# Expert and shared matrices laid out turned ahead of the launch and loaded into place, in a graph layer with routed experts

## The reference, cut to what matters

```python
def _L0_ffn_ref(x, gate_w, w1, w2, w3, sw1, sw2):      # 8 experts, 512 -> 256 -> 512
    logits = xf @ gate_w.T                             # one expert a token, weight 1
    h = silu(einsum('nd,eid->nei', xf, w1)) * einsum('nd,eid->nei', xf, w3)
    y = einsum('nei,edi->nd', h * comb[:, :, None], w2)
    y = y + gelu(xf @ sw1.T) @ sw2.T                   # the shared part
```

## Time and profile before

| | |
|---|---|
| median of 3 runs | 2850.24 us (2848.74 to 2852.52) |
| the profiled execution: span from first to last instruction | 3300.0 us |
| mean granted TensorE clock over the span | 0.919 |
| busy shares: PE, DVE, POOL, ACT | 77%, 67%, 46%, 22% |
| `route_and_share` in the trace | from 2964.3 us to the first gather of the experts at 3115.8 |
| `run_experts` in the trace | from 3115.8 us to the end |

### The profile page before, as it was taken

One profiled execution on the slowest core, in us unless ns is written; L12 is line 12 of the kernel. 1 busy time (PEld: TensorE's weight loads), 2 busy tenths in 40 slices (PEclk: granted clock), 3 DMA queues, 4 the chain that ended last, 5 costly groups with the idle time before them and its releaser, 6 DMA issues. The chain is left out here.

```text
span 3300.0 us, 44711 instructions
## 1 busy us (share of the span) xinstructions
PE 2528.1 (77%) x13652; PEld 1568.7 (48%) x13652; DVE 2222.5 (67%) x3894; ACT 731.3 (22%) x1526; POOL 1531.5 (46%) x1568
## 2 busy tenths in 40 slices
PE   3999894888888878888784067877877777887798
PEld 2565543555555555555553034444444444446443
DVE  7578543777777777777777967676766767775222
ACT  1333311333333333333332010000000000004321
POOL 2232203555555555555552056666655665641144
PEclk7999997999999999999997578988888888889899
DMA  3112227666666666666666045656555565654443
GB/s 125 47 60 63 73 93 134 175 177 174 174 173 175 177 173 174 174 175 176 174 173 205 34 143 168 176 167 173 168 166 171 164 173 164 177 149 154 133 128 94
DMA packets 180188, 490.81 MB, mean 149 GB/s; under 512 B 39490, under 2 KB 52194, under 8 KB 178942
## 3 DMA queue, kind: packets, MB, share of 16 engines
q0 software_dynamic: 117200, 384.69, 41.9%
q1 hardware_dynamic: 48468, 77.23, 7.7%
q10 hardware_dynamic: 14298, 26.03, 2.5%
HBM read 440.04 MB, written 49.72 MB: 148 GB/s over the span
## 5 line engine op out<-in xcount | busy, mean ns | idle before, releaser
L1078 POOL DMA_INDIRECT rows_v<-target_rows,edge_dst x672 | 682.6, 1016 | 682.8 <-ACT edge_terms L1184 423.7
L1405 PE MATMUL ps_sum<-messages,node_onehot 128*125 128x512 f32 x1344 | 806.7, 694 | 232.3 <-DVE messages L1381 221.5
L1360 POOL DMA_INDIRECT rows_e<-message_rows,edge_dst x672 | 635.7, 946 | 552.0 <-issue 204.7
L1095 DVE TENSOR_TENSOR rows_v<-rows_v,ps_u 128x520 f32<-128x520 f32 x672 | 451.3, 693 | 328.0 <-PE ps_u L1127 175.4
L1127 PE MATMUL ps_u<-edge_space,source_onehot_t 125*128 x4032 | 535.5, 277 | 55.5 <-DVE rows_v L1095 37.0
L1178 ACT ACTIVATE w_abs<-ps_w 128x1024 f32<-128x1024 f32 x336 | 344.2, 1024 | 845.8 <-remote 558.4
L1142 PE MATMUL ps_w<-ident,rows_v 128*128 128x128 f32 x2688 | 362.4, 278 | 212.3 <-ACT w_abs L1178 212.3
L1109 DVE SCALAR_TENSOR_TENSOR w_abs<-w_abs,corner 128x512 f32<-128x512 f32 x672 | 474.0, 746 | 0.9 <-ACT w_abs L1178 0.9
L1142 PEld LDWEIGHTS ps_w<-ident,rows_v 128*128 128x128 f32 x2688 | 292.4, 142 | 358.8 <-DVE rows_v L1095 280.6
L1127 PEld LDWEIGHTS ps_u<-edge_space,source_onehot_t 125*128 125x128 bf16 x4032 | 378.7, 97 | 152.4 <-issue 75.8
L1406 PEld LDWEIGHTS ps_den<-edge_space,node_onehot 128*125 128x125 f32 x1344 | 273.6, 204 | 368.8 <-issue 368.8
(11 more groups left out here) (404 smaller groups left out, 2366.7 us busy)
## 6 DMA issues: line engine op xcount, KB each, us to landing
edge_ids<-local_ids ACTq DMA_DIRECT2D x84, 250.0 KB
edge_space<-in_L_ffn_w_dram SPq DMA_DIRECT2D x24, 512.0 KB, 4.3
rows_v<-target_rows,edge_dst POOLq DMA_INDIRECT x672
scores<-score SPq DMA_DIRECT2D x672, 16.0 KB
rows_e<-message_rows,edge_dst POOLq DMA_INDIRECT x672
source_parts<-edge_space SPq DMA_DIRECT2D x20, 380.9 KB
edge_space<-source_parts SPq DMA_DIRECT2D x4, 1904.3 KB
scores<-score SPq DMA_DIRECT2D x336, 8.0 KB
```

Source lines behind the costliest of these rows:

```text
L1078: nc.gpsimd.indirect_dma_start(rows[q][:, j, :], None, tab_v, bass.IndirectOffsetOnAxis(ap=edge["dst"][:, tile:tile + 1], axis=0)).then_in ...
L1095: v.tensor_tensor(w[q % RING][:, j, :].rearrange("p (a b) -> p a b", a=2), rows[q % RING][:, j, :].rearrange("p (a b) -> p a b", a=2), ps_ ...
L1360: nc.gpsimd.indirect_dma_start(rows[q][:, j, :], None, tab_e, bass.IndirectOffsetOnAxis(ap=edge["dst"][:, tile:tile + 1], axis=0)).then_in ...
L1405: nc.tensor.matmul(ps_sum[h][:, :], onehot[h][:, j, :], messages[h][:, j, :], start=j == 0, stop=j == GROUP - 1)
```

## The change

`kernel()` now calls `lay_out`, which turns the six kinds of matrices before the launch and hands them over as four arrays: `up` (`w1` and `w3` side by side), `down`, `gate_up` (gate and `sw1` side by side) and `shared_down`, each with the partition first. In `route_and_share` SP loads them straight into the tiles that the products read: 27 loads become 8, of which the two of `down` wait until `sums`, whose space they take, has been used up. `turn_matrix` and `keep_matrix` are gone with their PSUM banks and places. PE waits for `gate_up` ahead of its first tile and for `shared_down` ahead of the second loop's first product; `run_experts` waits for all six expert loads (`experts_in`) between turning its first tile and the first product. The factor one half moves from the copies of `w2` to DVE's second gating operation, which changes its form for it.

```diff
         @block.sync
         def _(sp):
-            sp.dma_start(gate_rows, a["L0_ffn_gate_w"]).then_inc(s["gate_in"], 16)
-
-            def load(m):
-                name, e = MATRICES[m]
-                if m >= RAWS:
-                    sp.wait_ge(weights_turned, m - RAWS + 1)
...
-                sp.dma_start(rows, whole.rearrange("(k p) f -> p k f", p=P)).then_inc(loaded[m % RAWS], 16)
...
+            sp.dma_start(ffn["gate_up"][:, :, :], a["gate_up"]).then_inc(s["gate_up_in"], 16)
+            sp.dma_start(ffn["shared_down"][:, :, :], a["shared_down"]).then_inc(s["shared_in"], 16)
+            for k in range(KF):
+                sp.dma_start(ffn["up"][:, k, :, :], a["up"][:, k, :, :]).then_inc(experts_in, 16)
+            sp.wait_ge(s["sums_used"], NC)
+            for e in range(0, EXPERTS, EXPERTS // 2):
+                sp.dma_start(ffn["down"][:, e:e + EXPERTS // 2, :, :], a["down"][:, e:e + EXPERTS // 2, :, :]).then_inc(experts_in, 16)
+            sp.wait_ge(s["shared_in"], 16)
...
-            def turn_matrix(m):
-                pe.wait_ge(loaded[m % RAWS], 16 * (m // RAWS + 1))
-                if m >= 2:
-                    pe.wait_ge(weights_kept, m - 1)
-                for half in range(IH):
-                    for k in range(KF):
-                        at = k * INNER + half * P if wide(m) else half * F + k * P
-                        ins = t_.transpose(ps_w[2 * (m % 2) + half][:, k * P:(k + 1) * P], raw[m % RAWS][:, at:at + P], ident[:, :])
-                ins.then_inc(weights_turned, 1)
...
-            pe.wait_ge(s["gate_in"], 16)
-            for k in range(KF):
-                ins = t_.transpose(ps_gate[:, k * EXPERTS:(k + 1) * EXPERTS], gate_rows[:, k * P:(k + 1) * P], ident[0:EXPERTS, 0:EXPERTS])
-            ins.then_inc(s["gate_turned"], 1)
-            for m in range(BEFORE):
-                turn_matrix(m)
+            pe.wait_ge(s["gate_up_in"], 16)
...
-            act.wait_ge(s["gate_turned"], 1)
-            sc.copy(ffn["gate_up"][:, :, 0:EXPERTS], ps_gate[:, 0:KF * EXPERTS].rearrange("p (k e) -> p k e", k=KF))
-            for m in range(2):
-                keep_matrix(m)
-            for m in range(2, BEFORE):
-                keep_matrix(m)
             deviate(0)
...
-                v.tensor_tensor(hidden[:, :], ps_up[:, INNER:2 * INNER], gate[:, :], ALU.mult).then_inc(s["hidden_set"], 1)
+                v.scalar_tensor_tensor(hidden[:, :], ps_up[:, INNER:2 * INNER], 0.5, gate[:, :], ALU.mult, ALU.mult).then_inc(s["hidden_set"], 1)
...
             turn(0)
+            pe.wait_ge(experts_in, 16 * (KF + 2))
             up(0)
...
+def lay_out(inputs, np):
+    def turned(name):
+        return np.moveaxis(inputs[name], -1, 0)
+
+    def chunks(one):
+        return one.reshape((-1, P) + one.shape[1:]).swapaxes(0, 1)
+    up = np.concatenate([turned('L0_ffn_w1'), turned('L0_ffn_w3')], axis=2)
+    gate_up = np.concatenate([turned('L0_ffn_gate_w'), turned('L0_ffn_sw1')], axis=1)
+    down = np.moveaxis(chunks(turned('L0_ffn_w2')), 2, 1)
+    laid = {name: inputs[name] for name in _INS}
+    laid.update(up=chunks(up), gate_up=chunks(gate_up), down=down, shared_down=chunks(turned('L0_ffn_sw2')))
+    return laid
```

More of the change, by code:

```diff
@@ L1422, in _, with route_and_share @@
             in_turns(TURNS, ((0, lay_weights),), TURN)
[L1425 removed]
+def route_and_share(nc, a, const, ffn, x_sb, sums, denominators, spare, raw_space, idle, tokens, tab_x, tab_r, residual_out, experts_in):
     ident, tri, ones, row, eps = (const[k] for k in ("ident", "tri", "ones", "row", "eps"))
@@ L1508, in ps_h @@
             return ps_xt[(t - LISTED_AT) % 2 if t >= LISTED_AT + 2 else 1]
-        def matrices_at(first, last, step, steps):
-            share = last - first
-            return range(first + share * step // steps, first + share * (step + 1) // steps)
         @block.sync
         def _(sp):
-            sp.dma_start(gate_rows, a["L0_ffn_gate_w"]).then_inc(s["gate_in"], 16)
-            def load(m):
-                name, e = MATRICES[m]
-                if m >= RAWS:
-                    sp.wait_ge(weights_turned, m - RAWS + 1)
-                whole = a[name][e, :, :] if name in ("L0_ffn_w1", "L0_ffn_w2", "L0_ffn_w3") else a[name]
-                rows = raw[m % RAWS].rearrange("p (k i) -> p k i", k=KF) if wide(m) else raw[m % RAWS].rearrange("p (i f) -> p i f", f=F)
-                sp.dma_start(rows, whole.rearrange("(k p) f -> p k f", p=P)).then_inc(loaded[m % RAWS], 16)
-            for m in range(RAWS):
-                load(m)
-            for m in range(RAWS, len(MATRICES)):
-                load(m)
+            sp.dma_start(ffn["gate_up"][:, :, :], a["gate_up"]).then_inc(s["gate_up_in"], 16)
[6 more added lines that the diff above has]
+            sp.wait_ge(s["shared_in"], 16)
         @block.gpsimd
@@ L1821, in _, with run_experts @@
                         gelu(t + 2)
-                    for m in matrices_at(AT_COUNT + 3, len(MATRICES), t, NB):
-                        keep_matrix(m)
-def run_experts(nc, const, ffn, tokens, tab_x, tab_r, residual_out, out):
+def run_experts(nc, const, ffn, tokens, tab_x, tab_r, residual_out, experts_in, out):
     ident = const["ident"]
@@ L2040 @@
     arrays, args = {}, {}
-    for name in _INS:
-        a = _np.ascontiguousarray(inputs[name])
+    for name, laid in lay_out(inputs, _np).items():
+        a = _np.ascontiguousarray(laid)
         arrays[f"in_{name}_dram"] = a
```

62 lines of the change are left out of this document (10 added, 52 removed).

## The result

The changed kernel takes 2824.82 us (median of 4 runs, 2823.87 to 2825.24), the kernel before, run beside it, 2850.99 (4 runs, 2848.74 to 2852.52): a ratio of 0.991, 95% interval 0.9898 to 0.9922, or 26.2 us gained where 20.4 were forecast. The forecast of 2829.8 us is 5 us too high; its range of 2824.5 to 2839 holds the result by 0.3 us. It was right on the direction and on most of the steps. That the range holds is luck: its terms at their best gave 25.1 us, or 2825.1 us, and the result lies beyond that. Behind the missing 5 us stand errors with opposite signs. Writes that were held up cost some 3.6 us where nothing was taken. The half clock, which costs the kernel before more than its one trace showed and the change less than before, gave some 8 us that were not counted: some 2 in the start and 6 in the first loop. Smaller differences make up the rest.

What follows compares the result with a forecast made beforehand. The stage was taken as bound by a late start, an ACT-DVE-PE ring, DVE's routing, then PE in the second loop. 5.5 - 1.0 + 5.8 + 0.9 - 0.5 + 9.7 = 20.4 us off 2850.24 gives 2829.8, range 2824.5 to 2839.

Steps and rivals of the forecast that it cites:

- The start: Start of the stage: without the matrices' turning ahead of it, the first tile reaches PE earlier, 5.5 us gained.
- The loss by a cold PE at the start: First group: PE, idle for 14 us before, works at the half clock for a while, 1.0 us lost.
- The ring: First loop, through ACT, DVE and PE: four roots each come 1.46 us earlier without matrix copies, 5.8 us gained.
- The contention: First group's writes of normalized tiles beside the expert loads: at half the rate, 1.25 us each, costing nothing.
- rival 1: POOL's writes starve behind the large loads: 4.5 us lost, 2834.3; far end 2852; chance 0.10, of which 0.02 far end.
- The clock in the first loop: Whether slow groups at the half clock come none, two or four times is open: 3.2 us either way around nothing.
- Rival 2: First loop: PE falls to the half clock without its transposes, 28.6 us lost against 20.4 gained, 2858.4 us; chance 0.04.
- Routing and list: Removed matrices give nothing under DVE's chain; idle PE may run the counting products at the half clock, 0.5 us lost.
- The second loop: Loop of 20 tiles held by PE: eleven of twelve turned matrices leave its path, 0.88 us each, 9.7 us gained.
- the experts' loads: Ahead of the first expert product: PE's one new wait has some 70 us of cover and costs nothing.
- Rivals 3 and 4: 3: DVE bounds the first loop, 2835.6 us, chance 0.04; 4: expert loads not covered, around 2850, 0.04 with everything unseen.
- The 450 us between the trace and the runs: Profiled execution is 450 us longer than the runs' median; the stage's gain is carried over whole, 20.4 us.

Runs made afterwards that it cites:

- experiment 1: Kernel before, unchanged, in two more traces: 3312.41 and 3300.34 us; changed kernel, unchanged, two more times: 3283.98 us, ratio 0.9931, and 2826.05 us, ratio 0.991.
- the spread version: Changed kernel with the third and fourth load of `up` held until PE turned one and two groups: 3285.58 us, ratio 0.992; again 2823.31 us, ratio 0.9899.
- experiment 2: The spread version, and the changed kernel with `up` in 32 loads of 256 KB with rows of 2 KB: 3288.51 us, ratio 0.992.
- experiment 3: The spread version with one unread copy of 832 columns on ACT ahead of the roots of groups 2 to 5: 3290.52 us, one execution.
- experiment 5: The spread version with unread transposes in PE's idle time: 3275.93 us (0.9898) and 2821.42 (0.9899); with 44 instead of 24 ahead of the list: 2820.06 (0.989).
- experiment 4: Changed kernel with eight unread transposes put back at each of twelve places in the second loop, without loads or copies: 3298.81 us, ratio 0.9959.

## Why the prediction was right, and where it was not

**The start: right.** First tile forecast at 12.7 us behind the stage's start, measured 12.65 to 12.75 in all eleven traces of the new layout. The gain was larger than 5.5 us because the kernel before took 20.1 and 20.2 in its two later traces and not the 18.2 that the first showed, 2 us that are the half clock's (experiment 1). That term rested on one execution.

**The loss by a cold PE at the start: right in kind.** 1.0 us was taken. The first step was 11.45, 11.46 and 11.90 us in the change and 9.57 with PE kept at work: 1.9 to 2.3. But the kernel before paid for a half clock there as well, at 12.07, 13.19 and 13.56.

**The ring: right.** Undisturbed steps are 12.16 before and 10.60 after: 1.56 us each for 1.46.

**The contention: the step that failed first.** "With half of the rate they take 1.25 us each and cost nothing, which I take." The four writes took 8.5 to 13.0 us. The last place was freed at 2535.62, 27.8 us behind the stage's start, where the prediction's other end, behind everything on SP's queue, had said 28.2. The undisturbed steps sum to 42.40 us (10.69, 10.60, 10.59 and 10.52 in the spread version) and the change's to 47.17, 45.20 and 48.28. Of the difference some 2.3, 2.0 and 2.0 us are the second step's, by the writes, and 1.7, 0 and 2.7 the third's, by PE's idle time behind them. So rival 1 came true, at 2 to 4.7 us for its 4.5. The prediction had given it a tenth, and it was there in each of the four traces with a full queue of long rows. What misled was to share the rate evenly between the queues, with no row of before for it: the writes got 18% of the bytes (experiment 2).

From the Trainium skill's rule (the page and section above) the prediction had worked out a fifth, with the fourth write landing near 2991, and priced it against PE's want of the tile at 2995 instead of DVE's reuse of the place, which it had itself put at 2988. By its own numbers that was a wait of 2 to 3 us, and the three traces of the change have waits of 2.7 to 3.2 us.

**The clock in the first loop: the step that failed second, with the other sign.** The prediction held the number of half-clock stretches for chance, 3.2 us either way around nothing. It was not chance around the same mean. By PE's idle time ahead of groups 2 to 5, and the mean granted clock of the group:

| idle ahead | where | groups | of them below clock 1.00 |
|---|---|---|---|
| 0.6 to 0.9 us | PE filled | 12 | 0 |
| 1.46 to 1.54 | the new layout | 24, four of them held inside by waits for writes | 2 (0.94, 0.96), both of the four |
| 2.15 to 2.32 | before; and with the copy on ACT | 16 | 10 (0.87 to 0.88) |
| 3.56 to 3.97 | behind waits for writes | 4 | 3 (0.79 to 0.86) |

The shorter ring took these stretches away. The four steps of the kernel before were 4.5 us over 4 x 12.16 in the two later traces, and the fifth group, slow in each of three traces of before and in none of the change, gives 1.7 us of the 2.6 in the table. Rival 2, the half clock because PE has less to do, expected a busy share of 0.83 against 0.82 before; it came out at 0.86, and 0.94 with PE filled. The order of the table is thus also the order of the busy shares of undisturbed groups (0.94, 0.86, 0.80 to 0.82), and the groups ahead of the last row were busy 0.64 to 0.72. That the shorter ring brought the clock back is borne out by the copy on ACT, which lengthened it and had the half clock in two of four groups (experiment 3), though in one execution only. Whether the length of the idle piece or the share does it, no kernel here separates.

The Trainium skill (TensorE: Matmul & The Clock Gate, Part 1) has activity release the full rate. The rows agree: with transposes in the idle time ahead of them, the first group, the counting products and, with 44 transposes, the token list ran at the full clock (experiment 5).

**Routing and list: half right.** The counting products took 0.7 us longer in four of eight traces, and never with PE kept at work; 0.5 was taken. What was missed is the next place of the same kind: the eight transposes that stood ahead of the token list were said to fall into PE's wait and cost nothing, but without them the list runs at the half clock behind 4.32 us of idle time, and the step takes 5.86 us instead of 5.17. With eight transposes put back it took 4.68 (experiment 4), and with PE filled 3.71 (experiment 5).

**The second loop, the gating product, the experts' loads: right,** at 9.6 us for 9.7, 424 ns for 423, and no wait. Rivals 3 and 4 didn't come.

**The 450 us between the trace and the runs:** to carry the sum over whole was right. They lie ahead of the stage, and the stage takes the same time at both levels (131.5 and 132.1).

**The sum** as the later traces show it: 24.6 us in the stage and 0.8 in the experts' loop, against 26.2 measured, 22.2 to 29.1 by the interval. Without the contention it would have been some 3.6 more. No cause was looked for behind the 0.8. What stays open is why one execution of the same kernel has more of the half clock than another (1.8 us in the second loop's start of the change, 2 us in the start of before), and what of the idle time sets it.

## What to carry to other kernels

When many small loads become a few large ones, ask who else uses the DMA engines while they flow, and share the rate between the queues by the lengths of their packets, not evenly; then hold back what isn't needed yet, which costs one wait a load. Where work leaves PE, look at the idle time ahead of each stretch and at the busy share as it will be: a shorter ring can bring the clock back, and a filler removed from ahead of a wait can lose it. One trace is one draw: a second of the kernel before would have shown this stage 5 us longer.

## What the runs showed of the hardware beyond what was expected

A write of 250 KB that lands in 3 to 4 us took 8.5 to 13.0 beside loads in rows of 16 KB, and 6.0 to 7.1 beside as many bytes in rows of 2 KB. While both flowed, the DMA engines took about as many packets from the one queue as from the other (162 and 159; 245 and 248), so the longer packets got the bytes. PE's clock fell in 10 of 16 groups behind idle pieces of 2.2 us and in none of 20 behind 1.5 that weren't held up inside. A version with 136 additional transposes was the fastest of all, by 6.0 us against the change.
